# Two routed groups of batches in place of one early piece and a rest, with the closing loads of the first group issued among the blocks of the second

## The reference

```python
x = x + attention(layernorm(x))       # scores = Q K^T, times tril, times V; then @ wo.T + wo_b
xm = layernorm(x).reshape(-1, D)      # 4096 tokens
probs = softmax(xm @ Wg)
topk_p, topk_i = top_k(probs, 2)      # 8192 (token, expert) pairs
for e in range(E):
    ye = relu(xs @ W1[e] + b1[e]) @ W2[e] + b2[e]
y = y * p_sorted[:, None]
out = zeros.at[tok_idx].add(y)
return x + out
```

## Time and profile before

| | |
|---|---|
| time, three runs | 298.23, 298.89 and 353.44 us, median 298.89 |
| the profiled execution | 297.89 us, of which 296.1 us span |
| PE busy | 228.8 us (77%), weight loads 171.2 us |
| GpSimd busy | 204.5 us (69%) in 188 instructions |
| VectorE busy | 201.2 us (68%) |
| ScalarE busy | 142.4 us (48%) |
| DMA | 24.98 MB, mean 84 GB/s; over 300 GB/s only at the start and in the last two slices of 7.4 us |

### The profile page before, as it was taken

One profiled execution on the slowest core, in us unless ns is written; L12 is line 12 of the kernel. 1 busy time (PEld: TensorE's weight loads), 2 busy tenths in 40 slices (PEclk: granted clock), 3 DMA queues, 4 the chain that ended last, 5 costly groups with the idle time before them and its releaser, 6 DMA issues.

```text
span 296.1 us, 6311 instructions
## 1 busy us (share of the span) xinstructions
PE 228.8 (77%) x1392; PEld 171.2 (58%) x1392; DVE 201.2 (68%) x696; ACT 142.4 (48%) x509; POOL 204.5 (69%) x188
## 2 busy tenths in 40 slices
PE   0499999999999998988794399999997999840000
PEld 0244666666656565655573279988996989830000
DVE  7978889889898998989967485454443544410284
ACT  3234366646476463654444156666664757510000
POOL 3166568738889889889776777777777777777000
PEclk9999999999999999999955569999999999985555
DMA  6940000000100100100115532343333333211599
GB/s 203 312 101 0 0 3 0 3 1 20 38 26 29 39 27 28 38 27 28 49 53 114 132 101 74 98 111 97 97 104 98 106 97 104 82 49 34 184 358 309
DMA packets 32357, 24.98 MB, mean 84 GB/s; under 512 B 4388, under 2 KB 30252, under 8 KB 32322
## 3 DMA queue, kind: packets, MB, share of 16 engines
q1 hardware_dynamic: 23766, 14.01, 17.8%
q0 software_dynamic: 4320, 8.47, 8.8%
q10 hardware_dynamic: 4236, 2.10, 2.4%
HBM read 13.41 MB, written 11.61 MB: 84 GB/s over the span
## 4 chain that ended last, share of the span: by engine, by line
PE 49%; DVE 16%; issue 11%; DMA 11%; POOL 5%; ACT 2%; SPq 2%; ACTq 1%; POOLq 1%; DVEq 0%
PE ps L820 15%; PE ps L790 7%; PE ps L909 6%; PE ps L917 6%; POOL returned L397 5%; DMA returned<-y_sb,xt 4%; DMA back<-returned 4%; DVE o_sb L590 3%; DVE prod L577 3%; DMA xt<-dispatched 2%; PE ps L811 2%; PE ps L829 2%; SPq L323 2%; PE ps L840 2%; PE ps L792 2%
## 5 line engine op out<-in xcount | busy, mean ns | idle before, releaser
L397 POOL DMA_INDIRECT returned<-y_sb,xt x71 | 70.2, 989 | 21.7 <-issue 17.4
L358 POOL TENSOR_TENSOR outer<-qkv 128x1024 f32<-128x1024 f32 x32 | 62.5, 1954 | 27.3 <-ACT qkv L452 26.9
L388 POOL DMA_INDIRECT dispatched<-rows,slot x64 | 62.6, 978 | 18.9 <-issue 14.5
L820 PE MATMUL ps<-outer,causal 128*128 128x512 f32 x128 | 63.1, 616 | 0.0
L766 DVE TENSOR_SCALAR y_sb<-ps,xt 128x128 f32<-128x128 f32 x71 | 24.9, 350 | 45.3 <-PE ps L919 45.3
L909 PE MATMUL ps<-xT,w_of 128*128 128x128 f32 x284 | 48.7, 295 | 1.6 <-ACT xT L502 1.1
L917 PE MATMUL ps<-w_sb,hT 128*128 x284 | 44.7, 281 | 0.5 <-DVE y_sb L766 0.4
L508 ACT ACTIVATE hT<-ps,b_col 128x128 f32<-128x128 f32 x142 | 44.3, 365 | 0.9 <-PE ps L909 0.7
L577 DVE TENSOR_TENSOR prod<-ps,qkv 128x1024 f32<-128x1024 f32 x32 | 39.0, 1220 | 4.7 <-PE ps L820 4.7
L909 PEld LDWEIGHTS ps<-xT,w_of 128*128 128x128 f32 x284 | 38.5, 197 | 3.8 <-ACT xT L502 2.8
L590 DVE TENSOR_REDUCE o_sb<-prod 128x128 f32<-128x1024 f32 x32 | 38.7, 1210 | 0.1
(11 more groups left out here) (140 smaller groups left out, 385.7 us busy)
## 6 DMA issues: line engine op xcount, KB each, us to landing
xt<-dispatched SPq DMA_DIRECT2D x71, 65.0 KB, 1.9
back<-returned SPq DMA_DIRECT2D x8, 512.0 KB, 7.4
x_sb<-x SPq DMA_DIRECT2D x8, 256.0 KB, 4.6
out<-x_sb ACTq DMA_DIRECT2D x8, 256.0 KB, 6.6
returned<-y_sb,xt POOLq DMA_INDIRECT x71, 2.3
w_sb<-w SPq DMA_DIRECT2D x1, 1024.0 KB, 6.4
w_sb<-w SPq DMA_DIRECT2D x2, 512.0 KB, 7.4
dispatched<-rows,slot POOLq DMA_INDIRECT x64, 2.3
```

Source lines behind the costliest of these rows:

```text
L358: pool.tensor_tensor(outer[:, g % OUTER_RING, :].rearrange("p (h b a) -> p h b a", h=HEADS, b=DH), k, v, ALU.mult).then_inc(outer_done, 1)
L388: pool.indirect_dma_start(out=dispatched[:, :], out_offset=bass.IndirectOffsetOnAxis(ap=slot[:, g * K + k:g * K + k + 1], axis=0), in_=row ...
L397: pool.indirect_dma_start(out=returned[:, :], out_offset=bass.IndirectOffsetOnAxis(ap=xt[:, n % G, D:D + 1].bitcast(I32), axis=0), in_=y_s ...
L820: mm = pe.matmul(ps_run[g % 2][:, u, :], causal[:, :], outer[:, g % OUTER_RING, 512 * u:512 * (u + 1)], start=True, stop=True)
```

## The change

- **Groups.** The batches are two groups, 0 to 5 and 6 to 7, each with its own regions in `dispatched` and its own table. Each group's count starts at zero (`rank` leaves out the running count in batch 6, `before` in `softmax_end` does the same).
- **Blocks.** Group one has up to 48 full blocks, group two 16. A leftover of more than 64 rows takes a full block; any other leftover takes a half block of 64 rows. There are 8 + 8 half entries, two to a block: 48 full, 8 split blocks, 16 full, `BLOCKS = 72`, with 80 entries. In a split block SyncE issues two loads of 64 rows, VectorE copies two W1 and scales twice, TensorE runs W1 on 64 columns for each half and W2 and bias twice in full, ScalarE four relus on 64 columns. One send serves both halves.
- **Tables.** One function `table(i)` makes both; the first stands where the early table stood, the second where the final table stood. The first group's 8 paddings now stand ahead of the first load, which waits for them and for the dispatches of six batches.
- **Rings.** `G` is 20 in place of 16; the ring of copied W1 has 8 places in place of 4 and lies in the part of `back` that belongs to batches 6 and 7.
- **Closing.** `returned` holds a token row of a partition's four tiles side by side, so that a closing load reads 4 KB in one piece per partition in place of four pieces of 1 KB. The loads of batches 0 to 5 wait for the first 52 blocks and then for block 51, 54, 57, 60, 63, 66; those of batches 6 and 7 for all.
- Small: GpSimd's constants are made after the first and the second outer product, with 13 in place of 8.

```diff
-    REGION = TOKENS + P
+    HALF = P // 2
+    GROUPS = ((0, 6), (6, 8))
+    SEEN = GROUPS[0][1]
+    FULL = [(stop - first) * T * K for first, stop in GROUPS]
+    SPLIT = range(FULL[0], FULL[0] + E)
+    BLOCKS = FULL[0] + FULL[1] + E
+    FIRST_BLOCKS = FULL[0] + E // 2
-    G = 16
+    G = 20
     W = 4
+    W1_RING = 8
...
+        w1_of = back[:, SEEN * T * K * D:N * K * D].rearrange("p (w h) -> p w h", w=W1_RING)
...
-        back_t = returned.rearrange("(b t p k) d -> b p t (k d)", b=B, t=T, k=K)
+        back_t = returned.rearrange("(b p r) d -> b p (r d)", b=B, r=T * K)
...
-            for n in range(EARLY):
-                load_block(n)
...
+            pad_regions(0)
+            sp.wait_ge(pads_done, 16 * (2 + E))
+            sp.wait_ge(first_dispatch_done, 16 * SEEN * T * K)
+            for n in range(G):
+                load_block(n)
+            pad_regions(1)
+            for n in range(G, FIRST_BLOCKS):
+                load_block(n)
+            sp.wait_ge(pads_done, 16 * (2 + 2 * E))
+            sp.wait_ge(dispatch_done, 16 * (N - SEEN * T) * K)
+            for n in range(FIRST_BLOCKS, BLOCKS):
+                load_block(n)
+
+            for (first, stop), blocks in zip(GROUPS, (FIRST_BLOCKS, BLOCKS)):
+                for t in range(G):
+                    sp.wait_ge(return_done[t], 16 * returns(t, blocks))
+                for b in range(first, stop):
+                    paced_by = FIRST_BLOCKS - 1 + 3 * b if b < SEEN else BLOCKS - 1
+                    sp.wait_ge(return_done[paced_by % G], 16 * (paced_by // G + 1))
+                    sp.dma_start(back[:, b * T * K * D:(b + 1) * T * K * D], back_t[b]).then_inc(back_in[b], 16)
...
             def w1_out(n):
-                wait(dve, h_mm, n + 1 - W)
-                dve.tensor_copy(w1_of[:, n % W, :], w1_sb[:, bass.ds(w1_from[n], H)]).then_inc(w1_done, 1)
+                for entry in entries(n):
+                    if entry >= W1_RING:
+                        dve.wait_ge(h_mm, block_of(entry - W1_RING) + 1)
+                    dve.tensor_copy(w1_of[:, entry % W1_RING, :], w1_sb[:, bass.ds(w1_from[entry], H)]).then_inc(w1_done, 1)
...
             def output(n):
+                for i, entry in enumerate(entries(n)):
+                    for c in range(HC):
+                        pe.matmul(ps_y[n % 2][:, i, :], hT[:, n % W, c, :], w2_sb[:, c, bass.ds(w2_from[entry], D)],
+                                  start=(c == 0), stop=False)
+                    mm = pe.matmul(ps_y[n % 2][:, i, :], ones[:, :], b2_parts[:, bass.ds(w2_from[entry], D)], start=False, stop=True)
+                mm.then_inc(y_mm, 1)
```

More of the change, by code:

```diff
@@ L239, in states, with returns, pieces, entries @@
             return (T - 1) * (g // T) + g % T if g >= 0 else 0
-        def returns(t):
-            return (BLOCKS - t - 1) // G + 1
+        def returns(t, blocks):
+            return (blocks - t - 1) // G + 1
+        def pieces(n):
+            return n + min(max(n - SPLIT.start, 0), len(SPLIT))
+        def entries(n):
+            return range(pieces(n), pieces(n + 1))
+        def block_of(entry):
+            return next(n for n in range(BLOCKS) if entry in entries(n))
+        def loads(n):
+            return sum(len(entries(m)) for m in range(n % G, n + 1, G))
+        def rows_of(n, i):
+            return slice(i * HALF, (i + 1) * HALF) if n in SPLIT else slice(0, P)
+        def chunk(n):
+            first = pieces(n)
+            return range(first, first + READ) if first % READ == 0 else None
         def batches(g):
@@ L297, in _, with pad_regions @@
                 sp.dma_start(b2_parts[32 * part:32 * part + 1, :], piece[32 * part:32 * part + 1, :]).then_inc(b2_done, 16)
+            def pad_regions(i):
+                sp.wait_ge(end_row_done, i + 1)
+                for row in read(mybir.EngineType.SP, end_row[0:1, i, 0:E], PAD_BLOCK[i]):
+                    sp.dma_start(dispatched[bass.ds(row, P), :], padding[:, :]).then_inc(pads_done, 16)
             row_of = {}
             def load_block(n):
-                if n % READ == 0:
-                    row_of.update(enumerate(read(mybir.EngineType.SP, row_at[0:1, n:min(n + READ, BLOCKS)], PAD_BLOCK), n))
+                own = chunk(n)
+                if own is not None:
+                    sp.wait_ge(table_done[1 if n >= SPLIT.start else 0], 5)
+                    row_of.update(zip(own, read(mybir.EngineType.SP, row_at[0:1, own.start:own.stop], PAD_BLOCK[1])))
@@ L394, in send_back @@
             def send_back(n):
-                wait(pool, y_done, n + 1)
+                wait(pool, y_done, pieces(n + 1))
                 apart(pool)
@@ L893, in registers @@
             def registers(n):
[L894 to L897 removed]
+                own = chunk(n)
+                if own is not None:
+                    pe.wait_ge(table_done[1 if n >= SPLIT.start else 0], 5)
+                    w2_from.update(zip(own, read(mybir.EngineType.PE, w2_at[0:1, own.start:own.stop], (E - 1) * D)))
             def transpose_x(n):
[L900 removed]
+                pe.wait_ge(xt_in[n % G], 16 * loads(n))
                 wait(pe, xT_done, n - 1)
```

349 lines of the change are left out of this document (173 added, 176 removed).

## The result

The changed kernel takes 293.38 us (median of 4 runs, 293.01 to 293.88), the kernel before 298.33; the ratio is 0.983 with a 95% interval of 0.9804 to 0.9856. The 298.33 us are the median of the three fast runs of four, since one run of the kernel before took 353.44 us, in a slower state, and is left out. The change makes the kernel 1.7% faster, less than the 2% that count as a difference here. The forecast was 292.4. The profiled execution takes 293.01 us with a span of 291.3 against 296.1.

The account below looks back on a forecast made before the run. The prediction took GpSimd's queue from tile 24 on, then the closing, as the bound. 2.85 + 1.29 - 10.6 = -6.5 us gave 291.4, plus 1.0 from profiled execution to median: 292.4, range 290.2 to 296.5.

Parts of the forecast that it names:

- The bound: From tile 24's dispatch on, GpSimd's queue of dispatches and sends, then the closing of 22.99 us, set the time, not TensorE.
- Term 1: The first table on VectorE, ahead of batch 6's places, delays tile 24 and all GpSimd work behind it: +2.85 us.
- rival B of the late table: An experiment's rival: with the table moved, the wait shifts to batch 7's places; last send under 1 us earlier; no chance given.
- Term 2: GpSimd's sends: one more, 72 in place of 71, +1.29 us.
- The covers: First load, first result, middle blocks and split blocks all stay ahead of GpSimd's sends, so they cost nothing.
- The lead: How far VectorE's scaling of a block runs ahead of its send: 5.6 us at first, growing 0.18 a block.
- Term 3: The closing behind the last send's start takes 12.4 us in place of 22.99: -10.6 us.
- the closing loads do not get cheaper: Rival: early closing loads crowd the DMA engines; batch 5's load and store delay the last two loads, 293.5; chance 0.15.
- the forecast's own 290.8 to 293.3: The whole kernel's time if all work ahead of GpSimd's sends stays ahead: 290.8 to 293.3; chance 0.50.
- The adds that hold sends: Rival: in the closing, VectorE's adds hold GpSimd's sends, end up to 6.9 us later, 295 to 299; chance 0.08.
- Drained lead: Rival: split blocks take 3.5 us each, so sends wait 3 to 4 us, 294 to 298; chance 0.12.
- Slower: Rival: split blocks cost 4.6 us or more, sends starve for 12.5 us, 305; chance 0.05.

Follow-up runs that it names:

- late table: The changed kernel with the first group's table two slots later on VectorE, behind batch 6's places: 291.42 us, ratio 0.9756 to the kernel before.
- cut table: The changed kernel with the first group's table split: 7 instructions one slot earlier on VectorE, 19 behind batch 6's places: 291.21 us, ratio 0.9771.
- load per two blocks: The changed kernel with a closing load of the first group issued every two blocks in place of three: 291.22 us, ratio 0.976.
- the run with 0.9 us more: The changed kernel with each W1 matmul of the 8 split blocks run twice: 295.63 us, ratio 0.9918 to the kernel before.

## Why the prediction was right, and where it was not

**The bound** was read rightly. GpSimd's queue and the closing set the time, and TensorE's 77% did not: 7.1 us of further matmuls cost 2.3 us.

**Term 1**, +2.85 by the sum. The table took 5.28 us against the 5.1 counted, tile 24 starts 2.69 us later and the first send 2.50. The late and the cut table show that the table is the cause, since tile 24 is back at 162.04 and 161.25 without it. The working said that batch 7's places are needed 10 us later and so don't matter. That is true of the table where it stands, and false as soon as it is moved; rival B of the late table named it.

**Term 2**, +1.29: 72 sends, at 1.292 us each.

**The covers** held. The first load was early enough. A split block costs TensorE 2.07 us against the 2.1 worked out; its W1 matmuls on 64 columns take 0.90 us (238.33 to 239.23), where those on 128 take 0.50 (182.57 to 183.07):

```profile
238.33 1.06 PE L969 MATMUL ps<-xT,back 128*128 128x64 f32 x8
239.23 0.28 PE L960 MATMUL ps<-ident,xt 128*128 128x128 f32 x1
...
240.40 1.06 PE L969 MATMUL ps<-xT,back 128*128 128x64 f32 x8
```

The lead was put at 14 us at block 48 and 7 behind the split blocks; it was 9.8 and 5.2. The growth was 0.16 a block (6.4 at block 0, 12.7 at block 40) and not 0.18, and it stopped at block 43. TensorE waited 1.12 us for the load of a block at 229.00, and the scalings of the last full blocks stand behind the W1 matmuls of the first split ones. The second profile of the same kernel has no such wait for a load, and its lead is 11.1 at block 48 and 6.4 at block 55.

**Term 3** is the step that was mis-sized: -10.6 by the sum, -8.5 measured (14.5 us in place of 12.4).

| piece | sum | measured |
|---|---|---|
| last send's landing | 2.13 | 4.26 |
| SyncE's waits | 0.6 | 0.64 |
| first load | 3.8 | 4.11 |
| batch 6's adds or batch 7's load | 1.5 | 1.33 |
| batch 7's adds | 1.41 | 1.41 |
| last store | 2.93 | 2.76 |

The errors of the other pieces cancel, and what is left is the landing. The sum took 2.13 from an end at which nothing else was on the DMA engines. It had block 66's send landed by 273.2 and batch 5's load over by 277.5. But sends after 268 us land in 2.8 to 6.0 us (median 4.3) in the changed kernel, with batch 4's load and the first stores beside them. Block 66's send, started at 270.29, took 6.0 us to land; so batch 5's load, which waits for it, is issued at 276.26 and lies beside the last send, and batch 4's store does too. It is a loop: a load that waits for a send slows the next sends' landing, which delays the next load. The load per two blocks breaks it, with a landing of 2.25 us. The rival "the closing loads do not get cheaper" named this contention and gave 293.5, which is where the time came out: 293.38 lies just above the forecast's own 290.8 to 293.3. But the price is another one. The rival put it on the last two loads, and the first of these cost only 0.3 us more than the sum; what it left out is that the last send's own landing bears it, with 2.1 us. So that the rival's number fits is in part luck.

**Luck in the forecast's number.** The span came out 1.7 us above the sum (291.3 against 289.6), the median only 1.0 us above the forecast. The difference is the 1.0 us that was added for the way from the profiled execution to the median. It was read from a median of three runs of which one took 353.44 us, and in the changed kernel it is 0.4.

**The adds that hold sends.** They exist, and the prediction named a send beside adds that takes longer than 0.98 as a sign of being wrong. The cost is 0.30 for the first send and 0.04 for each of five more in the kernel with a load per two blocks, 0.5 in all, and 1.1 us in the second profile of the changed kernel, not up to 6.9. The rows of all runs follow one rule: a send that begins 0.05 to 0.54 us after the start of an add (42 sends in ten runs) ends 0.84 to 0.87 us after the add's end. Begun 0.05 us after the add it takes 1.50 us, at 0.11 it takes 1.44, at 0.27 it takes 1.28, at 0.46 it takes 1.09 and at 0.52 it takes 1.02; behind that it takes its 0.98. The Trainium skill, page "SBUF — State Buffer", section "SBUF: two separate sides", says that an operation of VectorE with two SBUF inputs and a GpSimd instruction that reads SBUF share an exclusive port pair, and that the second of the two waits for the first to end. For a send behind an add the trace agrees, since the send's end moves with the add's end and not with its own start. For an add behind a send it does not: adds that begin 0.08 us or more after a send's start take their 0.69 us. The cost is small by the way the two fall together: a pair of adds takes 1.33 us and a send 1.29, and once a send was held the next ones begin 0.52 us behind an add's start, where 0.04 us is all that is left to wait.

The prediction's working set this rule against a row in which a dispatch beside an operation on two SBUF operands took no longer, and that row can't tell: the dispatch started at 174.78, ahead of the operation at 175.10. The trace of the kernel before had rows that can, the copies of W1 (0.28 us, from SBUF to SBUF). VectorE's and GpSimd's timelines:

```profile
178.60 0.28 DVE L761 COPY w_of<-w_sb 128x256 f32 x1
178.63 1.08 POOL L388 DMA_INDIRECT dispatched<-rows,slot  x1 [0.30 <-issue]
```

The dispatch begins 0.03 us after the copy and takes 1.08 in place of 0.96, and it ends 0.83 us after the copy's end.

**The other rivals.** Drained lead: no send waited. Slower: it would have needed 4.6 us a split block. With the measured lead of 5.2 us at block 55, of which 0.9 is no cover, I estimate that the sends begin to wait when a split block is dearer by 4.3 / 8 = 0.54 us; the run with 0.9 us more lost 2.3.

## What to carry to other kernels

Where one queue of fixed-cost instructions runs through to the end, price a change by what it puts on that queue and by what stands behind its last item; work on busier engines is free up to the lead, which can be read block by block from two timelines. Transfers that are released by the landing of that queue's items slow the same landings, so release them early enough to be over before the last item, not evenly up to it. A table or other small-step work on a vector engine belongs in a slot where it idles, and before moving it, the next consumer's due time must be read too.

## What was not expected of the hardware

- An indirect DMA of 128 rows landed in 2.1 to 2.3 us at a quiet end (kernel before, and 2.26 without early loads) and in 3.3 to 4.3 us in the seven kernels with a load per three blocks, where batch 5's load of 512 KB and stores of 256 KB are beside it, whether this load read pieces of 4 KB (4.26 in the changed kernel) or of 1 KB (4.11). Beside one such store alone it landed in 2.56.
- Issuing a 512 KB load that stands alone on the queue costs SyncE 0.32 us with one piece per partition (changed kernel) and 0.36 with four (closing loads in pieces of 1 KB). In a row of eight it costs more: 0.39, 0.50 and up to 1.42 with four pieces (before), 0.33 to 0.66 with one (all closing loads at the end). The time did not move.
- An indirect DMA of GpSimd that begins 0.05 to 0.54 us after the start of one of VectorE's adds on two SBUF operands ends 0.84 to 0.87 us after the add's end and so is up to 0.52 us longer (1.50 for 0.98); an add that begins 0.08 us or more behind it is not held. A copy of W1 on VectorE, 0.28 us alone, is held: where it began 0.54 to 0.79 us after a send's start, it ended 1.09 to 1.11 us after that start, in all runs, and so took up to 0.56 us.
